# Stores that add onto rows laid beforehand, a fifth list level, and the last weighing on ScalarE, in an attention and mixture-of-experts kernel

## Chip, cores and metric

One Trainium2 chip, one core. The metric is the device time of one execution in microseconds, as the median of three runs.

## What is computed

Four sequences of 1024 tokens with 128 features, float32. A layer norm and an attention block are added onto the tokens, then a layer norm and a routed block of 8 experts, of which each token takes the best two:

```python
x = x + attention(layernorm(x))              # causal softmax, w_q, w_k, w_v, w_o
h = layernorm(x)                             # [4096, 128]
scores = softmax(h @ gate_w.T)               # 8 experts
top_scores, sel = top_k(scores, 2)
y[n, k] = (silu(h[n] @ w1[e]) * (h[n] @ w3[e])) @ w2[e]      # e = sel[n, k], H = 256
out = x + top_scores[:, 0] * y[:, 0] + top_scores[:, 1] * y[:, 1]
```

## The kernel before

**Attention.** The tokens lie in 32 tiles of 128 (`N_TILES`), in the SBUF tensor `X`, which is updated in place. A software pipeline of 32 steps does one tile a step. VectorE's `attend` (L1008) writes x + attention into `X` and raises `x1_rdy`, so `x1_rdy` 4(c+1) means that chunk c of four tiles is final. Every four tiles form a routing group (`GROUPS`, 8 of them). GpSimd's `scatter` (L524) sends each token's normalised row twice, once for each chosen expert, into the DRAM tensor `expert_rows`, where each expert has a stretch of its own: 64 indirect DMAs of 128 rows.

**The list.** Which 128 rows the expert loop takes at each of its steps is worked out on VectorE, on one partition. `LEVELS` names the groups after which rows are counted: the list takes first the whole tiles of rows that are there after group 4, then those after group 6, then the others. So a tile early in the list has only tokens of early groups, and their results are complete early. `list_full` writes the first 32 entries (`NT0`), `list_rest` the other 40 (`NT1`), from arrays `past` and `pasts` of 40 x `SEG` elements, with `SEG` = 8 x (number of levels) = 32. `list_rest` is cut into 7 parts that stand between VectorE's tile steps 8 to 18 (`REST_AT`).

**The expert loop.** 71 steps (`NT`), one for each tile of rows. In step t TensorE multiplies tile t by w1 and w3 (`up`, L747), turns tile t+4 (`pair`, L764), and multiplies the gated tile t-3 by w2 (L768). ScalarE stages the weights (L884) and takes the silu (L889). VectorE (`out_pair`) copies the turned tile, keeps the destinations and weights of tile t+4 in a ring `ycol` of 16 (`keep_places`, L1214, which waits until the store of tile t-12 has landed), weighs the result of tile t-3 into a ring `ysb` of 16 (L1226, `y_rdy`), and multiplies the gate (L1231). GpSimd's `store` (L535) sends `ysb` by an indirect DMA to `choice_rows`: 8192 rows, first those of choice 0 of each token, then those of choice 1, and rows behind them where padding goes. There are 65 stores (`STORED`). The results of the last 6 tiles are not stored: TensorE adds them onto the last three token tiles by a matrix of ones and zeros (`sow`, L691).

**The end.** SyncE's queue, in program order: the loads of rows (L395); `fetch(c)` of chunks 0 to 4, both choices, between the last five loads (L424, two DMAs of 256 KB a chunk); the writes of chunks 0 to 2 to the output (L429); a wait for the stores of the first 63 tiles and the fetches of chunks 5 and 6; a wait for all 65 and half of the last fetch (L346). ScalarE's queue: a wait for all stores, the other half of the last fetch (L346), and the writes of chunks 3 to 6 (L957). VectorE adds the fetched chunks to `X`, first choice 0 and then choice 1 (L1391, one instruction each), those of chunks 0 to 2 between its steps 59 to 64, the others behind the loop; then the sown sums (L1423, L1425) and the last chunk (L1432, L1435). The last writes are at L352.

Of the kernel before, what the change touches and what calls it, by code (L numbers as in the profile page):

```python
# [22 lines left out]
P = 128  # L23
B, S, D = 4, 1024, 128
# [34 lines left out]
ROWS_HALF = K * P * sum(n for _, n in GROUPS[:HALF + 1])  # L59
NT0 = (ROWS_HALF - E * (P - 1)) // P // LANES * LANES  # L60
NEAR = 16
FAR, LATER = 6, 63
SOWN = 3
LEVELS = (HALF, FAR, len(GROUPS) - 1, len(GROUPS) - 1)
SEG = len(LEVELS) * E
NT1 = LISTED - NT0
assert (ROWS_HALF + E * (P - 1)) // P - NT0 <= NEAR
assert (K * P * sum(n for _, n in GROUPS[:FAR + 1]) + E * (P - 1)) // P <= LATER
assert GROUPS[-1][1] > SOWN
N_PARTS = 5  # L70
REST_AT = [8, 9, 10, 12, 14, 16, 18]
# [16 lines left out]
CHUNKS = [(0, 2), (4, 4), (6, 4), (12, 4), (14, 4), (20, 4), (22, 4), (28, 2)]  # L88
N_EARLY, N_LATER = 5, 7
FETCH_AT = [66, 67, 68, 69, 70]  # L90
N_SOON, ADD_AT = 3, [59, 61, 63]
REST_OF = (STORED // OUT_LANES, STORED % OUT_LANES)


def pieces(c):

    a, apart = CHUNKS[c]
    return [(a, FIN)] if apart == 2 and c < NF - 1 else [(a, 2), (a + apart, 2)]
# [13 lines left out]
def build(nc, x, w_q, w_k, w_v, w_o, gate_w, w1, w2, w3, out):  # L112
# [9 lines left out]
    with ctx:  # L122
# [6 lines left out]
        def sem(name):  # L129
            return ctx.enter_context(nc.semaphore(name))  # L130
# [104 lines left out]
        head_mm, step_mm, xT_rdy, sil_rdy, g_rdy = (  # L235
            sem("head_mm"), sem("step_mm"), sem("xT_rdy"), sem("sil_rdy"), sem("g_rdy"))
        ycol_rdy = sem("ycol_rdy")
        Wt_rdy, y_rdy = sem("Wt_rdy"), sem("y_rdy")
        y_zero, low_rdy, lowf_rdy, pick_rdy, sown_mm = (
            sem("y_zero"), sem("low_rdy"), sem("lowf_rdy"), sem("pick_rdy"), sem("sown_mm"))  # L240
        sum2, last0, last1 = sem("sum2"), sem("last0"), sem("last1")
        assert NF - N_EARLY == LAG
        yf_in = [sem(f"yf_in{j}") for j in range(ZF)]
        sum0, sum1, out_done = sem("sum0"), sem("sum1"), sem("out_done")
        N_DESTS = 2 + (NF - 2) // 2
        N_CONST, N_PADS, M_TILES = 6, 11 + K * N_DESTS, LISTED // LANES


        ov = out.rearrange("b (i p) d -> p (b i) d", p=P)

        def is_tile(u):
            return 0 <= u < N_TILES
# [85 lines left out]
        def stores_in(eng, t0, t1):  # L338

            for q in range(OUT_LANES):  # L340
                if len(range(q, t1, OUT_LANES)) > len(range(q, t0, OUT_LANES)):
                    eng.wait_ge(y_out[q], 16 * len(range(q, t1, OUT_LANES)))
# [15 lines left out]
        def _(sp):  # L358
# [16 lines left out]
            for half, w in enumerate((w1, w3)):  # L375
# [4 lines left out]
            sp.wait_ge(pads_rdy, N_PADS)  # L380
            sp.dma_start(xs[E * STRETCH:XS_ROWS, :].rearrange("(j p) c -> p j c", p=P),
                         padrows[:, E:, :]).then_inc(padded, 16)
            for k in range(K):
                sp.dma_start(yv[:, k, LAST, :, :], padrows[:, 0:FIN, 0:D]).then_inc(y_zero, 16)

            def load(m, pads=(), between=False):
                _, firsts = nc.values_load_multi_w_load_instructions(
# [18 lines left out]
            rows_of(range(HALF + 1))  # L406
            sp.wait_ge(list_rdy, 1)
            load(0)
            with sp.Fori(1, M0 - 1) as m:
                load(m)  # L410

# [10 lines left out]
            def fetch(c):  # L422
                for k in range(K):
                    sp.dma_start(yf[:, c, k, :, :], yv[:, k, c, :, :]).then_inc(yf_in[c], 16)  # L424
# [15 lines left out]
                load(m)  # L440
            for m in range(FETCH_AT[0] // LANES, M_TILES):
                load(m, between=True)
            for c in range(N_SOON):
                write(c)
            stores_in(sp, 0, LATER)
            for c in range(N_EARLY, LAST):
                fetch(c)
            stores_in(sp, LATER, STORED)
            fetch_last(sp, 0)
            write_last(sp, 0)  # L450
# [4 lines left out]
        def _(pool):  # L455
# [72 lines left out]
            def store(r, q):  # L528

                pool.wait_ge(y_rdy, r * OUT_LANES + q + 1)  # L530
                if not isinstance(r, int):
                    pool.sem_inc(held, 1)
                    pool.wait_ge(step_mm, r * OUT_LANES + q + 2 + LAG)
                    pool.sem_inc(held, 1)
                nc.gpsimd.indirect_dma_start(  # L535
                    yb, bass.IndirectOffsetOnAxis(ap=ycol[:, q, 0:1].bitcast(u32), axis=0),
                    ysb[:, q, :], None).then_inc(y_out[q], 16)

            waiting = []
            pad_constants()  # L540
# [40 lines left out]
            for n in range(turn, turn + len(waiting) + NT0):  # L581
                after_tile(n)
                if (n - turn) % 5 in (0, 2) and waiting:
                    scatter(*waiting.pop(0))
                elif stored < NT0:
                    if stored == 0:
                        pool.wait_ge(y_zero, 16 * K)
                    store(stored // OUT_LANES, stored % OUT_LANES)
                    stored += 1
            with pool.Fori(NT0 // OUT_LANES, REST_OF[0] - 1) as r:  # L590
# [7 lines left out]
        def _(pe):  # L598
# [85 lines left out]
            def sow(t):  # L684

                n = t - STORED
                pe.wait_ge(y_rdy, t + 1)
                pe.wait_ge(pick_rdy, n + 1)
                for i in range(SOWN):
                    a, at = sown_at(i)  # L690
                    o = mm(a[:, at:at + D], pick[n][:, i * P:(i + 1) * P], ysb[:, t % OUT_LANES, :],  # L691
                           start=n == 0 and at == 0, stop=n == BY_PE - 1, skip_group_check=True)
                if n == BY_PE - 1:
                    o.then_inc(sown_mm, 1)
# [55 lines left out]
            def pair(m, j, w):  # L750

                static, t = isinstance(m, int), m * LANES + j
                b = bank[pair_bank(t if static else LANES + j)]
                used = pair_before(t) if static else t - RING
                if static and used is None:
                    pe.wait_ge(*((xT_rdy, 2 * t + 2) if t < 2 else (x1_rdy, N_TILES - 1) if b is pO else (place_rdy, NG)))
                elif static and used < LAG:
                    pe.wait_ge(xT_rdy, used + LEAD + 1)
                else:
                    pe.wait_ge(y_rdy, used - LAG + 1)  # L760
                if not static or t < LAST_TURN:
                    n = (j + LEAD) % LANES
                    pe.wait_ge(xt_in[n], 16 * (m + (j + LEAD) // LANES + 1))
                    i = nc.tensor.transpose(b[:, 0:P], xt[:, n, 0:D], identf[:, :])  # L764
                if not static or t >= LAG:
                    pe.wait_ge(g_rdy, t - LAG + 1)
                    for c in range(H // P):
                        i = mm(b[:, P:P + D], g[:, (j - LAG) % RING, c * P:(c + 1) * P], w2_sb[:, ds(w + c * D, D)],  # L768
                               start=c == 0, stop=c == H // P - 1)
                i.then_inc(step_mm, 1)  # L770
# [70 lines left out]
        def _(act):  # L841
# [102 lines left out]
                    silu(m, j)  # L944
            w = weights_of(M_TILES - 1, LANES - AHEAD)
            last = NT - (M_TILES - 1) * LANES
            for j in range(last):
                if j + AHEAD < last:
                    stage(M_TILES - 1, j + AHEAD, w[j])
                silu(M_TILES - 1, j)  # L950

            stores_in(act, 0, STORED)
            fetch_last(act, 1)
# [8 lines left out]
        def _(dve):  # L962
# [253 lines left out]
            def out_pair(r, q):  # L1216

                t = r * OUT_LANES + q
                b = bank[pair_bank(t if isinstance(r, int) else OUT_LANES + q % RING)]
                dve.wait_ge(step_mm, t + 1)  # L1220
                if not isinstance(r, int) or t < LAST_TURN:
                    v.tensor_copy(xT[:, (q + LEAD) % RING, :], b[:, 0:P]).then_inc(xT_rdy, 1)
                    keep_places(r + (q + LEAD) // OUT_LANES, (q + LEAD) % OUT_LANES)
                if not isinstance(r, int) or t >= LAG:
                    n = (q - LAG) % OUT_LANES
                    v.tensor_scalar(ysb[:, n, :], b[:, P:P + D], ycol[:, n, 1:2], None, ALU.mult).then_inc(y_rdy, 1)  # L1226

# [152 lines left out]

            pairs = X[:, :, 0:D].rearrange("p (n t) d -> p n t d", t=2)

            def add_choice(c, k):

                a, apart = CHUNKS[c]
                Xc = pairs[:, a // 2:a // 2 + apart // 2 + 1:apart // 2, :, :]
                if k == 0:
                    dve.wait_ge(yf_in[c], 16 * K)
                else:
                    dve.wait_ge(sum0, c + 1)  # L1390
                v.tensor_tensor(Xc, Xc, yf[:, c, k, :, :].rearrange("p (n t) d -> p n t d", t=2),  # L1391
                                ALU.add).then_inc([sum0, sum1][k], 1)

            for t in range(LANES, OUT_LANES + LAG):
                tile_step(0, t)
# [4 lines left out]
                    tile_step(r, q)  # L1400
            for t in range(NT0 + NEAR + LAG, NT):
                tile_step(t // OUT_LANES, t % OUT_LANES)
                for k in range(K):
                    if t - k in ADD_AT:
                        add_choice(ADD_AT.index(t - k), k)
                if t == NT - LEAD - 1:
                    low_places()
                for n in range(2):
                    if STORED <= STORED + 2 * (t - NT + LEAD) + n < NT:
                        picks(STORED + 2 * (t - NT + LEAD) + n)  # L1410
            out_pair(*divmod(NT, OUT_LANES))
            add_choice(N_SOON, 0)
            out_pair(*divmod(NT + 1, OUT_LANES))
            add_choice(N_SOON, 1)
            out_pair(*divmod(NT + 2, OUT_LANES))
            for c in range(N_SOON + 1, LAST):
                for k in range(K):
                    add_choice(c, k)

            n1 = N_TILES - SOWN  # L1420
            dve.wait_ge(sown_mm, 1)
# [37 lines left out]
```

## Time and profile before

| | us |
|---|---|
| median of 3 runs | 239.3 (238.39 to 239.92) |
| the profiled execution's own time | 239.59 |
| its span, first to last instruction | 237.8 |
| TensorE busy | 225.1 (95%) |
| VectorE busy | 187.6 (79%) |
| GpSimd busy | 163.3 (69%) |
| ScalarE busy | 145.8 (61%) |

The profiled execution is 1.8 us longer than its span and 0.3 us over the median. Engines are PE (TensorE), PEld (its weight loads), DVE (VectorE), ACT (ScalarE), POOL (GpSimd) and SP (SyncE). The mean granted clock of TensorE is 0.994 of full speed.

### The profile page before, as it was taken

How to read it: one execution, taken by the hardware profiler on the slowest of the kernel's cores; microseconds unless marked ns; L12 is line 12 of the kernel's file. 1: busy time of each engine (PE TensorE's matmuls, PEld its weight loads, DVE VectorE, ACT ScalarE, POOL GpSimd, SP SyncE). 2: the span in 40 equal slices, each digit the busy share in tenths (PEclk: the TensorE clock that was granted, in tenths of full speed). 3: DMA queues.
4: the chain of work that ended last, by engine and by line, in shares of the span. 5: the costliest groups of instructions: out<-in, count | busy, mean ns of one | idle time of the engine just before them, and what ended most of it. 6: DMA issues, size and time to landing. Idle time of an engine off the chain costs nothing.

```text
span 237.8 us, 6363 instructions
## 1 busy us (share of the span) xinstructions
PE 225.1 (95%) x1794; PEld 206.4 (87%) x1795; DVE 187.6 (79%) x851; ACT 145.8 (61%) x391; POOL 163.3 (69%) x204
## 2 busy tenths in 40 slices
PE   7989999999999999999999999999999999999960
PEld 6978888898799767877999998889999999999960
DVE  2479898879897789977898799957675656699994
ACT  2267787777877757855699665556575656566300
POOL 6523337788888888868577777777777777777700
PEclk9999999999999999999999999999999999999997
DMA  7999801111111111115124425534333333598368
GB/s 224 305 320 335 234 5 36 36 37 46 34 50 36 48 40 41 46 37 136 37 75 108 108 82 129 127 96 124 94 110 103 101 90 102 165 331 274 102 192 276
DMA packets 31978, 28.95 MB, mean 122 GB/s; under 512 B 4152, under 2 KB 26560, under 8 KB 31952
## 3 DMA queue, kind: packets, MB, share of 16 engines
q1 hardware_dynamic: 25216, 18.60, 28.5%
q0 software_dynamic: 4128, 8.59, 10.8%
q10 hardware_dynamic: 2608, 1.45, 2.0%
q8 instruction: 12, 0.20, 0.4%
q14 instruction: 14, 0.11, 0.2%
HBM read 16.34 MB, written 12.29 MB: 120 GB/s over the span
## 4 chain that ended last, share of the span: by engine, by line
PE 79%; POOL 6%; DMA 5%; DVE 3%; ACT 2%; issue 2%; ACTq 1%; POOLq 1%
PE scores L747 12%; PE turned L747 12%; PE scores L619 12%; PE weighed L680 11%; PE scores L768 6%; PE turned L645 5%; POOL expert_rows L524 4%; PE mixed L768 3%; PE weighed L768 3%; PE mixed L634 3%; PE mixed L633 3%; DMA choice_rows<-ysb,ycol 2%; DMA TL<-choice_rows 2%; DMA TL<-L_attn_w_o 2%; PE scores L764 2%
## 5 line engine op out<-in xcount | busy, mean ns | idle before, releaser
L535 POOL DMA_INDIRECT choice_rows<-ysb,ycol x65 | 65.0, 999 | 19.8 <-issue 14.6
L524 POOL DMA_INDIRECT expert_rows<-rows,slots x64 | 64.4, 1007 | 18.2 <-issue 13.2
L884 ACT ACTIVATE Wt<-W 128x512 f32 x71 | 44.1, 625 | 15.7 <-issue 15.7
L747 PE MATMUL scores<-xT,Wt 128*128 128x128 f32 x288 | 38.2, 276 | 0.8 <-issue 0.8
L619 PE MATMUL scores<-XX,TL 128*128 128x512 f32 (+3 forms) x96 | 38.1, 506 | 0.2 <-ACT TL L857 0.2
L680 PE MATMUL weighed<-TL,PT 128*128 128x136 f32 x272 | 37.0, 281 | 0.8 <-DVE X L1008 0.7
L747 PE MATMUL turned<-xT,Wt 128*128 128x128 f32 x280 | 37.1, 275 | 0.0
L747 PEld LDWEIGHTS scores<-xT,Wt 128*128 128x128 f32 x288 | 35.0, 192 | 1.1 <-issue 1.1
L680 PEld LDWEIGHTS weighed<-TL,PT 128*128 128x128 f32 x272 | 33.7, 190 | 1.7 <-issue 1.6
L747 PEld LDWEIGHTS turned<-xT,Wt 128*128 128x128 f32 x280 | 34.1, 192 | 0.0
L996 DVE TENSOR_REDUCE negmax<-scores 128x1 f32<-128x128 f32 (+7 forms) x32 | 23.5, 734 | 5.0 <-PE scores L619 5.0
L873 ACT ACTIVATE Pr<-scores,negmax 128x128 f32<-128x128 f32 (+7 forms) x32 | 23.9, 746 | 3.8 <-DVE negmax L996 3.5
L470 POOL TENSOR_TENSOR rstd<-ve,halves 128x1 f32<-128x1 f32 x32 | 19.2, 601 | 9.4 <-DVE ve L1021 8.9
L857 ACT ACTIVATE TL<-mixed 128x264 f32<-128x264 f32 x31 | 12.1, 391 | 20.8 <-PE mixed L634 20.5
L768 PE MATMUL scores<-w_sb,g 128*128 x156 | 24.1, 277 | 0.1
L867 ACT ACTIVATE PT<-turned 128x512 f32<-128x512 f32 (+3 forms) x48 | 21.9, 492 | 2.4 <-PE turned L645 2.4
L619 PEld LDWEIGHTS scores<-XX,TL 128*128 128x128 f32 x96 | 15.7, 191 | 8.6 <-issue 7.6
L889 ACT ACTIVATE sil<-turned 128x256 f32<-128x256 f32 x35 | 13.5, 385 | 15.1 <-PE scores L768 9.2
L645 PE MATMUL turned<-identf,Pr 128*128 128x128 f32 x144 | 21.1, 273 | 0.3 <-ACT Pr L873 0.3
L768 PEld LDWEIGHTS scores<-w_sb,g 128*128 128x128 f32 x156 | 20.5, 191 | 0.6 <-issue 0.3
L889 ACT ACTIVATE sil<-scores 128x256 f32<-128x256 f32 x36 | 13.6, 378 | 10.1 <-PE scores L768 6.1
L1231 DVE TENSOR_TENSOR g<-sil,scores 128x256 f32<-128x256 f32 x36 | 14.8, 412 | 5.5 <-ACT sil L889 5.5
(182 smaller groups left out, 456.1 us busy)
## 6 DMA issues: line engine op xcount, KB each, us to landing
xt<-expert_rows SPq DMA_DIRECT2D x71, 66.0 KB
TL<-choice_rows SPq DMA_DIRECT2D x15, 256.0 KB, 3.9
W<-L_ffn_w SPq DMA_DIRECT2D x2, 1024.0 KB, 9.7
out<-X ACTq DMA_DIRECT2D x9, 128.0 KB
choice_rows<-ysb,ycol POOLq DMA_INDIRECT x65, 2.3
X<-L_attn_in_features SPq DMA_DIRECT2D x2, 512.0 KB, 7.5
expert_rows<-rows,slots POOLq DMA_INDIRECT x64
out<-X SPq DMA_DIRECT2D x5, 128.0 KB
```

The costliest lines, as they stand in the source:

```text
L524: nc.gpsimd.indirect_dma_start(xs, bass.IndirectOffsetOnAxis(ap=slots[:, u, k:k + 1], axis=0), rows[:, u % ROWS_RING, k, :], None).then_in ...
L535: nc.gpsimd.indirect_dma_start(yb, bass.IndirectOffsetOnAxis(ap=ycol[:, q, 0:1].bitcast(u32), axis=0), ysb[:, q, :], None).then_inc(y_out[ ...
L619: i = mm(pS[u % 2][:, c:c + n * P], TL[:, token_tile(u), 0:P], keys, start=not last, stop=True, skip_group_check=last)
L645: i = nc.tensor.transpose(pT[n % 2][:, kt % 4 * P:(kt % 4 + 1) * P], Pr[:, u % 2, kt * P:(kt + 1) * P], identf[:, :])
L680: i = mm(weighed(u), PT[:, u % 2, kt * P:(kt + 1) * P], TL[:, first_key(u) + kt, P:], start=kt == 0, stop=kt == blocks(u) - 1)
L747: mm(bank[2 + j % RING][:, c * P:(c + 1) * P], Wt[:, j % RING, c * P:(c + 1) * P], xT[:, j % RING, :], start=True, stop=True)
L768: i = mm(b[:, P:P + D], g[:, (j - LAG) % RING, c * P:(c + 1) * P], w2_sb[:, ds(w + c * D, D)], start=c == 0, stop=c == H // P - 1)
L867: copy(PT[:, u % 2, 4 * c * P:4 * c * P + w], pT[n % 2][:, 0:w], ACT.Copy).then_inc(pt_ev, 1)
L873: copy(Pr[:, u % 2, 0:w], pS[u % 2][:, 0:w], ACT.Exp, bias=negmax[:, u:u + 1], scale=1.0, accum_out=rowsum[:, u:u + 1]).then_inc(p_rdy, 1)
L884: copy(Wt[:, j % RING, :], W[:, ds(w * (SET // WIDE), SET)], ACT.Copy).then_inc(Wt_rdy, 1)
L889: copy(sil[:, j % RING, :], bank[2 + j % RING][:, 0:H], ACT.Silu).then_inc(sil_rdy, 1)
L996: v.tensor_reduce(negmax[:, u:u + 1], pS[u % 2][:, 0:blocks(u) * P], AX.X, ALU.max, negate=True).then_inc(max_rdy, 1)
```

## The change

- **Stores that add.** `store` gets `compute_op=ALU.add`: the DMA adds onto the row that is there. For this SyncE lays rows beforehand. The residual of chunks 0 to 6 goes from `X` into the rows of choice 0 as soon as attention has finished a chunk (`lay_residual`, 13 DMAs, 1.75 MB in all), chunks 0 to 4 ahead of the first row load, 5 and 6 behind the first eight. Zeros go into the rows of choice 1, the padding rows and the last chunk's choice 0 (3 DMAs of 1 MB and one of 256 KB, where there were two of 256 KB). GpSimd's first store waits for all of these.
- **One addition a chunk.** `add_choices` writes `X` = fetched choice 0 + fetched choice 1, one instruction where there were two.
- **A list level.** `LEVELS` gets group 5 (`MID`): `SEG` is 40, the arrays in `list_rest` have 1600 elements instead of 1280, and chunk 5 is complete once 55 tiles are stored (`SOONER`).
- **Order at the end.** SyncE fetches chunk 5 right behind the last load and a wait for 55 tiles, then writes chunks 0 to 4, waits for 63 tiles and fetches chunk 6. ScalarE's queue writes chunks 5 and 6 alone.
- **ScalarE weighs sown tiles.** The results of tiles 65 to 70 are weighed by ScalarE (`weigh_sown`, `ys_rdy`), ahead of its wait for the stores and its half of the last fetch. VectorE's `out_pair` has nothing left to do in those steps.

```diff
+MID, SOONER = 5, 55
-LEVELS = (HALF, FAR, len(GROUPS) - 1, len(GROUPS) - 1)
+LEVELS = (HALF, MID, FAR, len(GROUPS) - 1, len(GROUPS) - 1)
-N_SOON, ADD_AT = 3, [59, 61, 63]
+N_SOON, ADD_AT = 5, [59, 61, 63, 65, 67]
...
+        ZERO_ROWS = (E + SPARE) * P
+        ZERO_AT = range(N_TOK, YB_ROWS, ZERO_ROWS)
...
-            for k in range(K):
-                sp.dma_start(yv[:, k, LAST, :, :], padrows[:, 0:FIN, 0:D]).then_inc(y_zero, 16)
+            sp.dma_start(yv[:, 0, LAST, :, :], padrows[:, 0:FIN, 0:D]).then_inc(y_zero, 16)
+            for n in ZERO_AT:
+                sp.dma_start(yb[n:n + ZERO_ROWS, :].rearrange("(j p) d -> p j d", p=P),
+                             padrows[:, :, 0:D]).then_inc(y_zero, 16)
+
+            def lay_residual(c):
+
+                sp.wait_ge(x1_rdy, (c + 1) * FIN)
+                for n, z in pieces(c):
+                    i = 0 if n == CHUNKS[c][0] else 2
+                    sp.dma_start(yv[:, 0, c, i:i + z, :], X[:, n:n + z, 0:D]).then_inc(y_base, 16)
+
+            for c in range(HALF + 1):
+                lay_residual(c)
...
             load(0)
+            for c in range(HALF + 1, LAST):
+                lay_residual(c)
...
+            stores_in(sp, 0, SOONER)
+            fetch(MID)
             for c in range(N_SOON):
                 write(c)
-            stores_in(sp, 0, LATER)
-            for c in range(N_EARLY, LAST):
-                fetch(c)
+            stores_in(sp, SOONER, LATER)
+            fetch(FAR)
...
-                    ysb[:, q, :], None).then_inc(y_out[q], 16)
+                    ysb[:, q, :], None, compute_op=ALU.add).then_inc(y_out[q], 16)
...
-                        pool.wait_ge(y_zero, 16 * K)
+                        pool.wait_ge(y_zero, 16 * (1 + len(ZERO_AT)))
+                        pool.wait_ge(y_base, 16 * sum(len(pieces(c)) for c in range(LAST)))
...
+            def weigh_sown(t):
+
+                at = t + LAG
+                act.wait_ge(ycol_rdy, t + 1)
+                act.wait_ge(step_mm, at + 1)
+                copy(ysb[:, t % OUT_LANES, :], bank[pair_bank(at)][:, P:P + D], ACT.Copy,
+                     scale=ycol[:, t % OUT_LANES, 1:2]).then_inc(ys_rdy, 1)
...
+                if t - LAG >= STORED:
+                    weigh_sown(t - LAG)
+            for t in range(NT - LAG, NT):
+                weigh_sown(t)
...
-            def add_choice(c, k):
+            def add_choices(c):
...
-                if k == 0:
-                    dve.wait_ge(yf_in[c], 16 * K)
-                else:
-                    dve.wait_ge(sum0, c + 1)
-                v.tensor_tensor(Xc, Xc, yf[:, c, k, :, :].rearrange("p (n t) d -> p n t d", t=2),
-                                ALU.add).then_inc([sum0, sum1][k], 1)
+                dve.wait_ge(yf_in[c], 16 * K)
+                y0, y1 = (yf[:, c, k, :, :].rearrange("p (n t) d -> p n t d", t=2) for k in range(K))
+                v.tensor_tensor(Xc, y0, y1, ALU.add).then_inc(sum1, 1)
```

## Rows read from the trace of the kernel before

**Rows 1.** The page: the span, and the chain that ended last, by engine.
```profile
span 237.8 us, 6363 instructions
...
PE 79%; POOL 6%; DMA 5%; DVE 3%; ACT 2%; issue 2%; ACTq 1%; POOLq 1%
```

**Rows 2.** The chain in order of time, its last pieces: start, length, what.
```profile
224.39 4.85 DMA choice_rows<-ysb,ycol
...
229.26 4.30 DMA TL<-choice_rows
...
234.84 0.42 DVE X L1435
```

**Rows 3.** Timeline of GpSimd: start, length, instruction, idle before it.
```profile
123.20 1.03 POOL L524 DMA_INDIRECT expert_rows<-rows,slots  x1 [0.19 <-issue]
...
132.12 0.96 POOL L535 DMA_INDIRECT choice_rows<-ysb,ycol  x1 [0.31 <-DVE ysb L1226]
...
138.43 2.08 POOL L535 DMA_INDIRECT choice_rows<-ysb,ycol  x1 [0.30 <-issue]
...
142.07 1.97 POOL L535 DMA_INDIRECT choice_rows<-ysb,ycol  x1 [0.30 <-issue]
...
145.61 0.95 POOL L524 DMA_INDIRECT expert_rows<-rows,slots  x1 [0.30 <-issue]
...
224.39 1.03 POOL L535 DMA_INDIRECT choice_rows<-ysb,ycol  x1 [0.30 <-issue]
```

**Rows 4.** Timeline of VectorE, read as Rows 3.
```profile
107.58 0.36 DVE L1008 SCALAR_TENSOR_TENSOR X<-weighed,rinv,X 128x136 f32<-128x136 f32 x1 [0.31 <-issue]
...
138.20 1.47 DVE L1128 TENSOR_TENSOR past<-cum,iotat 1x1280 f32<-1x1280 f32 x1
...
141.73 1.48 DVE L1138 TENSOR_TENSOR pasts<-past,step 1x1280 f32<-1x1280 f32 x1
...
144.96 1.47 DVE L1142 TENSOR_REDUCE e_of<-past 1x40 f32<-1x1280 f32 x1
...
156.83 0.17 DVE L1214 COPY ycol<-xt 128x2 f32<-128x2 f32 x1 [2.03 <-DMA choice_rows<-ysb,ycol]
...
220.75 0.35 DVE L1226 TENSOR_SCALAR ysb<-scores,ycol 128x128 f32<-128x128 f32 x1
...
228.11 0.35 DVE L1226 TENSOR_SCALAR ysb<-scores,ycol 128x128 f32<-128x128 f32 x1 [0.17 <-PE scores L768]
228.38 4.07 DVE L1391 TENSOR_TENSOR X<-X,TL 128x512 f32<-128x512 f32 x6
```

**Rows 5.** Instructions and waits on the rows of the choices (their tile), all of them.
```profile
L535 POOL DMA_INDIRECT choice_rows<-ysb,ycol x65: 954/958/2077, 132.1 to 224.4; - x65
...
  DVE ycol L1214: 6.1, 10
...
DMA to landing us min/median/max: 2.2/2.6/5.2
```

**Rows 6.** The scatters of the other indirect form: shortest, median and longest in ns.
```profile
L524 POOL DMA_INDIRECT expert_rows<-rows,slots x64: 954/961/1208, 36.6 to 154.5; - x64
```

**Rows 7.** Timeline of TensorE, the first part of two steps in a row.
```profile
206.16 1.06 PE L747 MATMUL turned<-xT,Wt 128*128 128x128 f32 x8
...
207.61 1.06 PE L747 MATMUL turned<-xT,Wt 128*128 128x128 f32 x8
```

**Rows 8.** Timeline of the queues that issue DMAs, SyncE first, then ScalarE.
```profile
224.15 1.79 SPq L424 DMA_DIRECT2D TL<-choice_rows  x4
...
229.69 4.40 ACTq L957 DMA_DIRECT2D out<-X  x8
```

**Rows 9.** DMA issues from 220 us on: GB/s in 40 slices of 0.45 us, size and time to landing.
```profile
GB/s 246 244 0 0 146 0 0 146 0 0 146 64 278 323 291 351 278 241 323 196 132 32 55 36 36 168 346 344 359 344 343 344 340 344 344 288 320 74 0 0
...
TL<-choice_rows SPq DMA_DIRECT2D x5, 256.0 KB, 3.7
```

**Rows 10.** One line of ScalarE: copies of 128x128 out of PSUM.
```profile
L846 ACT ACTIVATE XX<-scores x32: 259/278/298, 10.2 to 103.6; 128x128 f32<-128x128 f32 x32
```

More of the change, by code:

```diff
@@ L67 @@
 assert (ROWS_HALF + E * (P - 1)) // P - NT0 <= NEAR
-assert (K * P * sum(n for _, n in GROUPS[:FAR + 1]) + E * (P - 1)) // P <= LATER
+assert all((K * P * sum(n for _, n in GROUPS[:l + 1]) + E * (P - 1)) // P <= most for l, most in ((MID, SOONER), (FAR, LATER)))
 assert GROUPS[-1][1] > SOWN
@@ L237, in build @@
         ycol_rdy = sem("ycol_rdy")
-        Wt_rdy, y_rdy = sem("Wt_rdy"), sem("y_rdy")
+        Wt_rdy, y_rdy, ys_rdy = sem("Wt_rdy"), sem("y_rdy"), sem("ys_rdy")
         y_zero, low_rdy, lowf_rdy, pick_rdy, sown_mm = (
@@ L241, in build @@
         sum2, last0, last1 = sem("sum2"), sem("last0"), sem("last1")
-        assert NF - N_EARLY == LAG
+        assert MID == HALF + 1 == N_EARLY and FAR == NF - 2
         yf_in = [sem(f"yf_in{j}") for j in range(ZF)]
-        sum0, sum1, out_done = sem("sum0"), sem("sum1"), sem("out_done")
+        y_base, sum1, out_done = sem("y_base"), sem("sum1"), sem("out_done")
         N_DESTS = 2 + (NF - 2) // 2
@@ L249, in build @@
         ov = out.rearrange("b (i p) d -> p (b i) d", p=P)
+        ZERO_ROWS = (E + SPARE) * P
+        ZERO_AT = range(N_TOK, YB_ROWS, ZERO_ROWS)
+        assert (YB_ROWS - N_TOK) % ZERO_ROWS == 0
         def is_tile(u):
@@ L686, in sow @@
                 n = t - STORED
-                pe.wait_ge(y_rdy, t + 1)
+                pe.wait_ge(ys_rdy, n + 1)
                 pe.wait_ge(pick_rdy, n + 1)
@@ L758, in pair @@
                     pe.wait_ge(xT_rdy, used + LEAD + 1)
+                elif not static or used - LAG < STORED:
+                    pe.wait_ge(y_rdy, used - LAG + 1)
                 else:
-                    pe.wait_ge(y_rdy, used - LAG + 1)
+                    pe.wait_ge(ys_rdy, used - LAG - STORED + 1)
                 if not static or t < LAST_TURN:
@@ L946, in _ @@
             last = NT - (M_TILES - 1) * LANES
+            def weigh_sown(t):
[4 more added lines that the diff above has]
+                     scale=ycol[:, t % OUT_LANES, 1:2]).then_inc(ys_rdy, 1)
             for j in range(last):
+                t = (M_TILES - 1) * LANES + j
                 if j + AHEAD < last:
@@ L1223, in out_pair @@
                     keep_places(r + (q + LEAD) // OUT_LANES, (q + LEAD) % OUT_LANES)
-                if not isinstance(r, int) or t >= LAG:
+                if not isinstance(r, int) or LAG <= t < STORED + LAG:
                     n = (q - LAG) % OUT_LANES
@@ L1402, in _ @@
                 tile_step(t // OUT_LANES, t % OUT_LANES)
-                for k in range(K):
-                    if t - k in ADD_AT:
-                        add_choice(ADD_AT.index(t - k), k)
+                if t in ADD_AT:
+                    add_choices(ADD_AT.index(t))
                 if t == NT - LEAD - 1:
@@ L1410, in _ @@
                         picks(STORED + 2 * (t - NT + LEAD) + n)
[L1411 to L1418, printed above, removed]
+            for c in range(N_SOON, LAST):
+                add_choices(c)
             n1 = N_TILES - SOWN
```

## The prediction

> **What bounds the kernel now.** I read the page first. Its chain gives 79% of the span to PE [rows 1], but a share over the whole span says nothing of the end, so I then read the chain in order of time. Its last pieces name no TensorE work [rows 2]: the 65th store starts at 224.39 us and takes 4.85 us to land, the last fetch follows at 229.26 and takes 4.30, then come the last additions (to 235.26) and a write that ends the span at 237.8.
>
> What sets the start of the last store? VectorE had its data ready at 220.75 + 0.35 = 221.1 us [rows 4], 3.3 us before. So it waited for GpSimd. The timeline of GpSimd shows why: from 123.20 to 224.39 + 1.03 = 225.42 it issues 80 indirect DMAs, 15 scatters and all 65 stores, without one idle gap over 0.31 us [rows 3], and 102.2 / 80 = 1.28 us each, where one takes 0.96 and the gap that the profile calls issue takes 0.30. TensorE's step is 207.61 - 206.16 = 1.45 us [rows 7]. GpSimd fell behind while it had scatters beside stores, and has not quite caught up when the last store goes. **GpSimd's queue is the path of the last store**, and every nanosecond that a store gains costs 65 at the end. TensorE's path lies beside it: the last result of the loop is weighed at 228.11 us [rows 4].
>
> A second contact: the ring of 16. VectorE waited 10 times, 6.1 us in all, for a store to land before it could keep new places [rows 5], the longest 2.03 us, to 156.83 [rows 4]. So a store that lands later moves VectorE, and then TensorE, from there on.
>
> **Part 1, stores that add: GpSimd's time.** The trace holds no adding DMA. Its two indirect forms, rows of 528 and of 512 bytes, take the same 0.961 and 0.958 us [rows 5, 6], so the number of rows seems to set the time, not the bytes, and the rows stay 128. Lower bound 0: the same instruction with one more field has nothing to make it shorter. Upper bound: two DMAs during VectorE's long list operations show how much of the instruction is real work (next part): about 0.84 of its 0.96 us. Were this work half as long again, the extra would be 0.42 us. I take 0, the value of the two rows nearest to it, and keep the rest as a rival, for it is multiplied by 65.
>
> **Part 2, stores that add: landing.** A store lands 2.2 us after its start at the quickest (the median of 2.6 in that row holds the fetches too) [rows 5]; this DMA must now also read the DRAM row before it writes. A fetch, which reads DRAM, lands in 3.7 us [rows 9], of which 256 KB at 344 GB/s are 0.75, so 3.0. The extra lies between 0 and 3.0 - 2.2 = 0.8, or 1.6 if read and write follow each other wholly. I take 0.8. It hits twice: the last store lands 0.8 later, and VectorE's ring wait ends 0.8 later, which TensorE follows, since GpSimd's pace (1.26) is faster than TensorE's (1.45) only afterwards.
>
> **Part 3, the list level.** `list_rest` has four operations of 1280 elements at 1.47 us [rows 4]; at 1600 they take about 1.84, so VectorE has 4 x 0.37 + one more small operation, 1.7 us, more to do between 138 and 153 us. This lies in front of the 2.03 us that VectorE waited for a store, and is covered by it. But two of the four hold GpSimd up: the store at 138.43 starts inside the TENSOR_TENSOR of 138.20 to 139.67 and takes 2.08 us, the one at 142.07 inside that of 141.73 to 143.21 and takes 1.97, while the scatter at 145.61, inside the TENSOR_REDUCE of 144.96, takes 0.95 [rows 3, 4]. Both delayed stores end 0.83 to 0.84 us after VectorE's instruction does. So the two-input list operations each add their extension to the GpSimd queue: 2 x 0.37 = **+0.7 us** on the path of the last store. It depends on where a store happens to start in them: with a store every 1.26 us the sum lies between -1.3 and +1.2.
>
> **Part 4, laying rows.** Zeros: 3.25 MB behind the weight loads, at 344 GB/s [rows 9] 9.4 us of DMA time, in the early attention, where no load is waited for after that. Residuals: 13 DMAs of 128 or 256 KB over 80 us. The last of them needs 28 finished tiles, which attention has at 107.58 + 0.36 [rows 4]; the first store starts at 132.12 [rows 3], so its new waits cost nothing with 24 us of cover. On SyncE the row loads behind `lay_residual` wait for the expert loop's first steps anyway. I take 0 for all of it.
>
> **Part 5, the additions and ScalarE's weighing.** VectorE loses 7 additions of 4.07 / 6 = 0.68 us, 4.8 us [rows 4], and six weighings. None is on the chain: the additions behind the loop end at 232.45, before the last fetch lands at 233.56. Worth nothing by itself. ScalarE pays some 0.28 us a weighing [rows 10] for VectorE's 0.35 and has the time. But one thing moves: ScalarE issues its half of the last fetch **behind** its last weighing, which waits for TensorE's last product. Before, that product was weighed on another engine. So the last fetch now also waits for TensorE's path.
>
> **Part 6, the tail's transfers.** Before, 1 MB of fetches started at 224.15 [rows 8], beside the last store, which took 4.85 us instead of 2.2; the slices show the burst from 225.4 to 229 us [rows 9]. Now half of it, chunk 5, is fetched eight stores earlier. At 344 GB/s 0.5 MB are 1.5 us that the last store need not share. The writes on ScalarE's queue fall from 1 MB to 0.5 MB; the first 0.5 MB still run beside the last fetch, so of the 4.30 us I take off 0.4.
>
> **The sum.** The last store starts 0.7 later (part 3), at 225.1, and lands after 4.85 - 1.5 + 0.8 = 4.15, at 229.2, as before. TensorE's path: the wait at 156.83 ends 0.7 + 0.8 = 1.5 us later, TensorE with it; its last product is done at about 228.1 + 1.5 = 229.6, weighed by 229.9, and ScalarE's half of the last fetch goes at 229.95, against 229.26. It lands after 3.9, at 233.85 against 233.56. So the span grows by 0.3 us, to 238.1: the gain of part 6 is eaten by parts 2, 3 and 5. Profiled time 239.59 + 0.3 = 239.9; the median of the runs was 0.3 under the profiled one, so **239.6 us**. With the low ends (no extra landing, a favourable place for the two stores), the last fetch goes at about 228.6 and the time is 238.0; with the high ones (1.6 and 1.2, TensorE 2.8 later, the fetch at 231.25, minus 0.4) it is 241.0.
>
> **Rival A, GpSimd pays for the add.** Place: each of the 65 stores of the back-to-back queue. The last store decides again as soon as it lands after ScalarE's last weighing, a margin of 0.75 us, so from 0.75 / 65 = 12 ns a store. Price: 239.6 + 65 d - 0.75. With d = 0.07 us, the step between the 0.96 and 1.03 rows [rows 3], 243.4; with d = 0.25, the longest scatter of 1.208 [rows 6], 255; with d = 0.42, 266. Against: the two forms that are equal; for: the 0.84 us of real work must contain whatever is written for each row. The Trainium skill (Collectives: The Full Stack, on the DMA's adding unit) says that such an add takes two reads, and that two read descriptors are emitted for each piece in place of one. By that rule the work per row would be nearer to three parts than two, which is the 266 us end; no row here shows it.
>
> **Rival B, all goes well.** The add costs nothing anywhere and the list operations miss the stores: 238.0 as above, or 237.6 if the fetches land in 3.3. More than 1% would need the last fetch to be issued before 227.2, and TensorE's last product at 228.1 forbids it.
>
> **Rival C, adds that land slowly.** Each of the 16 DMA engines serves 8 rows of a store. Were reading and writing back not overlapped, landing could grow by several us; each us beyond mine moves TensorE and the end by one: 3 us give 242.
>
> **Chances.** What a measurement of this kernel can tell from no change is about 1%. Forecast 0.50, at 238.0 to 241.0; A 0.28; B 0.12; C 0.10. Less than 237.6 I hold for 0.07, by something I don't see. A spreads from 242 to 266, more of it low, so up to 252 takes in all but about 0.14. Range 237.6 to 252. Faster by over 1% (under 236.9) 0.10; within 0.57; slower (over 241.7) 0.33, from A, most of C and a little of the forecast.
>
> **What the profile after would show.** GpSimd's line of the store: median 0.96 us (right) or more (rival A). Landing: 3.0 at the quickest in place of 2.2. Stores or scatters near 138 and 142 us of some 2.4 us. Two fetches at about 225 us instead of four, a last store that lands in some 4.1 us. ScalarE's half of the last fetch issued after SyncE's. VectorE idle before the last additions. I am wrong if the store line is longer, if VectorE waits for landings all through the loop, or if the first store waits for laid rows.

## The result, and the profile after

The changed kernel takes **277.75 us** (276.5 to 278.51, 4 runs) against 239.24 of the kernel before: ratio 1.158, 95% interval 1.153 to 1.163, 38.5 us slower. My 239.6 and the range to 252 were wrong.

The page of the kernel after; section 5's columns are line, engine, instruction, tiles and count, then busy us and mean ns, then the idle time before it and what ended most of it:

```profile
span 276.4 us, 6390 instructions
...
q0 software_dynamic: 11408, 8.59, 21.4%
...
PE 38%; DMA 20%; POOL 16%; issue 13%; DVE 9%; ACT 2%; POOLq 1%; SPq 0%; DVEq 0%
...
L555 POOL DMA_INDIRECT choice_rows<-ysb,ycol x65 | 101.8, 1566 | 19.8 <-issue 14.0
...
L1251 DVE COPY ycol<-xt 128x2 f32<-128x2 f32 x71 | 12.4, 179 | 43.2 <-DMA choice_rows<-ysb,ycol 43.2
```

The store has become L555. It is the same instruction with the add, its mean is 1566 ns, and TensorE's share of the chain falls from 79% [rows 1] to 38%. VectorE waits 43.2 us for stores to land, where it waited 6.1 [rows 5].

Timeline of GpSimd after (the 1st, the 33rd and the last store):

```profile
133.70 1.62 POOL L555 DMA_INDIRECT choice_rows<-ysb,ycol  x1 [0.30 <-DVE ysb L1263]
...
203.81 1.55 POOL L555 DMA_INDIRECT choice_rows<-ysb,ycol  x1 [0.30 <-issue]
...
263.82 1.55 POOL L555 DMA_INDIRECT choice_rows<-ysb,ycol  x1 [0.30 <-issue]
```

All stores of the changed kernel, by their tile:

```profile
L555 POOL DMA_INDIRECT choice_rows<-ysb,ycol x65: 1554/1554/1902, 133.7 to 263.8; - x65
...
DMA to landing us min/median/max: 3.2/3.3/6.7
```

The median went from 958 [rows 5] to 1554 ns, **0.596 us more for each**. From the first store to the last it was 224.39 - 132.12 = 92.3 us [rows 3] and is now 263.82 - 133.70 = 130.1, 37.9 more; 64 x 0.596 = 38.1. The gap before each is 0.30 as before, and no gap between the first store and the last is over 0.31: the queue is back to back from end to end. So the size of the loss is all but explained; the first store also starts 1.6 us later, and the last one lands 0.7 us sooner after its start. TensorE's mean granted clock fell too, from 0.994 to 0.966, but it is 1.00 from 133 to 204 us, where the first half of the loss arises, so the clock is not what sets it.

The end of the chain in order of time, after:

```profile
263.82 4.13 DMA choice_rows<-ysb,ycol
...
267.97 4.45 DMA TL<-choice_rows
...
273.69 0.42 DVE X L1462
```

It has the shape of [rows 2], 39.4 us later: 4.85 us of landing have become 4.13, and 4.30 of the last fetch 4.45.

### The profile page after: what moved, and what is told of

It is laid out like the page before. It is cut to its first block, busy times and chain, and to the rows that moved or that the text cites. A ratio compares the mean times of both kernels' runs of the same rounds, so it can differ in the third digit from the quotient of the medians.

```text
span 276.4 us, 6390 instructions
## 1 busy us (share of the span) xinstructions
PE 238.0 (86%) x1795; PEld 211.4 (76%) x1796; DVE 184.3 (67%) x840; ACT 148.8 (54%) x397; POOL 201.6 (73%) x204
## 3 DMA queue, kind: packets, MB, share of 16 engines
q0 software_dynamic: 11408, 8.59, 21.4%
## 4 chain that ended last, share of the span: by engine, by line
PE 38%; DMA 20%; POOL 16%; issue 13%; DVE 9%; ACT 2%; POOLq 1%; SPq 0%; DVEq 0%
DMA choice_rows<-ysb,ycol 16%; POOL choice_rows L555 11%; PE scores L640 8%; PE weighed L701 8%; POOL expert_rows L544 4%; PE turned L666 4%; DMA TL<-choice_rows 3%; PE scores L768 3%; PE turned L768 3%; PE mixed L655 2%; PE mixed L654 2%; PE scores L791 1%; DMA TL<-L_attn_w_o 1%; DVE ysb L1263 1%; PE mixed L728 1%
## 5 line engine op out<-in xcount | busy, mean ns | idle before, releaser
L555 POOL DMA_INDIRECT choice_rows<-ysb,ycol x65 | 101.8, 1566 | 19.8 <-issue 14.0
L544 POOL DMA_INDIRECT expert_rows<-rows,slots x64 | 66.0, 1031 | 18.2 <-issue 13.5
L768 PE MATMUL scores<-xT,Wt 128*128 128x128 f32 x288 | 40.3, 285 | 5.6 <-issue 5.6
L768 PEld LDWEIGHTS scores<-xT,Wt 128*128 128x128 f32 x288 | 36.7, 199 | 6.8 <-issue 6.8
L1251 DVE COPY ycol<-xt 128x2 f32<-128x2 f32 x71 | 12.4, 179 | 43.2 <-DMA choice_rows<-ysb,ycol 43.2
L640 PE MATMUL scores<-XX,TL 128*128 128x512 f32 (+3 forms) x96 | 38.1, 506 | 0.2 <-ACT TL L880 0.2
L791 PE MATMUL scores<-w_sb,g 128*128 x156 | 26.6, 294 | 4.5 <-DVE g L1268 4.0
L791 PEld LDWEIGHTS scores<-w_sb,g 128*128 128x128 f32 x156 | 21.3, 198 | 8.6 <-issue 8.6
```

Of the source, the lines that this page charges most:

```text
L544: nc.gpsimd.indirect_dma_start(xs, bass.IndirectOffsetOnAxis(ap=slots[:, u, k:k + 1], axis=0), rows[:, u % ROWS_RING, k, :], None).then_in ...
L555: nc.gpsimd.indirect_dma_start(yb, bass.IndirectOffsetOnAxis(ap=ycol[:, q, 0:1].bitcast(u32), axis=0), ysb[:, q, :], None, compute_op=ALU. ...
L640: i = mm(pS[u % 2][:, c:c + n * P], TL[:, token_tile(u), 0:P], keys, start=not last, stop=True, skip_group_check=last)
L768: mm(bank[2 + j % RING][:, c * P:(c + 1) * P], Wt[:, j % RING, c * P:(c + 1) * P], xT[:, j % RING, :], start=True, stop=True)
```

## The experiments

They ran in three sessions, on the chips that the record numbers 7, 4 and 7; it doesn't number the chip of the result above ("first session" below). In these three sessions the kernel before takes 264 to 267 us (medians of 17, 29 and 29 runs) instead of 239. The kernels of one session are compared with its own before; why the level differs is looked at under "before_again".

### Only the add taken out, and only the add put in

plain_stores:

```diff
-                    ysb[:, q, :], None, compute_op=ALU.add).then_inc(y_out[q], 16)
+                    ysb[:, q, :], None).then_inc(y_out[q], 16)
```

> The kernel after with one thing undone: the stores copy instead of adding, everything else (laying rows, list level, order at the end, ScalarE's weighing) stays. It leaves out the residual and overwrites the laid rows. Theory 1, GpSimd's time per adding store (1.554 us against 0.958 in the two traces, 65 stores in a back-to-back queue, 38.7 us): 238 to 241 us, store line back at 0.96 us. Rival, the other parts carry a share of the 38.5 us: 245 us or more.

Measured: 264.35 us against 264.03 of before, ratio 1.000 (0.997 to 1.003). The store's median is back at 962 ns. Laying rows, the fifth level, the new order and ScalarE's weighing cost nothing that can be measured where before takes 264. The absolute 238 to 241 was missed, since before itself is at 264 here.

zeros_and_add, the kernel before with:

```diff
-            for k in range(K):
-                sp.dma_start(yv[:, k, LAST, :, :], padrows[:, 0:FIN, 0:D]).then_inc(y_zero, 16)
+            for n in range(0, YB_ROWS, (E + SPARE) * P):
+                sp.dma_start(yb[n:n + (E + SPARE) * P, :].rearrange("(j p) d -> p j d", p=P),
+                             padrows[:, :, 0:D]).then_inc(y_zero, 16)
...
-                        pool.wait_ge(y_zero, 16 * K)
+                        pool.wait_ge(y_zero, 16 * (YB_ROWS // ((E + SPARE) * P)))
...
-                    ysb[:, q, :], None).then_inc(y_out[q], 16)
+                    ysb[:, q, :], None, compute_op=ALU.add).then_inc(y_out[q], 16)
```

> The kernel before with one thing done: all rows of the choices are zeroed beforehand and the stores add; VectorE's additions, list, fetches and writes as before. Theory 1: 239.2 + 65 x 0.596 = 278 us, give or take 2. Rival, the other parts carry a share: under 270.

Measured: 280.03 us, ratio 1.060 (1.051 to 1.068). The add alone brings the time to that of the whole change, and to the time expected from a before of 239, in a session where before is at 264. There before is only 16 us faster. So the queue of adding stores gives nearly one time whatever before takes, and the 264 is another limit, which it overtakes.

### Is it the length of the queue, or the landing?

longer_queue, the kernel before with plain stores and

```diff
+                if not isinstance(r, int) or r * OUT_LANES + q > 0:
+                    pool.wait_ge(spent, r * OUT_LANES + q)
+                nc.gpsimd.tensor_tensor(extra[:, 0:1], ve1[:, 0:1], halves[:, 0:1], ALU.pow).then_inc(spent, 1)
                 nc.gpsimd.indirect_dma_start(
```

> The kernel before with plain stores, and one GpSimd instruction of about 0.6 us (a power of 128x1 elements, result unused) ahead of each store. Theory 1, what counts is how long GpSimd's queue is, not what the DMA does: about 239.2 + 65 x 0.6 = 278 us, with VectorE waiting some 40 us for landings although a store lands as fast as before. Rival, theory 2, the adding DMA lands later (median 3.3 us against 2.3) and the ring of 16 hands that on: 239 to 241 us, hardly any wait.

Measured: 278.5 us, ratio 1.054 (1.046 to 1.062). GpSimd's timeline, and from the view of the stores' tile who waited for it:

```profile
200.93 0.57 POOL L538 TENSOR_TENSOR extra<-ve,halves 128x1 f32<-128x1 f32 x1
201.69 1.03 POOL L539 DMA_INDIRECT choice_rows<-ysb,ycol  x1 [0.20 <-POOL extra L538]
...
203.52 1.03 POOL L539 DMA_INDIRECT choice_rows<-ysb,ycol  x1 [0.19 <-POOL extra L538]
```
```profile
  DVE ycol L1218: 41.0, 42
```

A store every 203.52 - 201.69 = 1.83 us, nearly as after (1.86), without any add; and VectorE "waits for the DMA" 41.0 us in 42 pieces. That is the sign that the changed kernel shows (43.2), and it comes here without an adding DMA: the store it waits for was late in the queue. (The trace has no landing times of these stores.) With the back-to-back queue of the kernel after, in which no store waits for a landing, the landing theory is out.

small_dose, the same with `nc.gpsimd.memset(extra[:, :], 0.0)` on 128x128 elements in place of the power:

> The kernel before with a small GpSimd instruction (a memset of 128x128, about 0.2 us) ahead of each store. Where the queue is the bound (before at 239), every 0.1 us that the instruction adds to a store's turn costs 6.5 us: some 10 to 15 us. Where before is at 264, the queue has slack of about 25 us beside it, so nothing or up to 5 us.

Measured: 267.99 us against 267.08, ratio 1.002 (0.999 to 1.005). Two stores in a row were 205.07 - 203.72 = 1.35 us apart:

```profile
203.72 0.97 POOL L539 DMA_INDIRECT choice_rows<-ysb,ycol  x1 [0.16 <-POOL extra L538]
...
205.07 0.97 POOL L539 DMA_INDIRECT choice_rows<-ysb,ycol  x1 [0.17 <-issue]
```

A turn is 0.09 us longer than the usual 1.26, not 0.2 as expected, since the gap before the store shrinks. That is some 6 us of queue, and they disappear (at most 1.3 us by the interval): here the queue has idle time.

### What an add costs, form by form

prices, the kernel before with 24 DMAs behind its last store:

```diff
+            def form(dest, at, n, c, **kw):
+                nc.gpsimd.iota(place[:, :], [[1, 1]], base=at, channel_multiplier=1).then_inc(placed, 1)
...
+                nc.gpsimd.indirect_dma_start(
+                    dest, bass.IndirectOffsetOnAxis(ap=place[0:n, 0:1], axis=0),
+                    ysb[0:n, 0, 0:c], None, **kw).then_inc(formed, 16)
+                pool.wait_ge(formed, 16 * n_form[0])
+            for rep in range(3):
+                form(wide_rows, 0, P, D)
+                form(wide_rows, 0, P, D, compute_op=ALU.add)
...
```

> The kernel before with 24 indirect DMAs behind the last store, one at a time, to DRAM rows of their own: copying and adding, each at 128, 64 and 32 rows of 512 bytes and at 128 rows of 128 bytes, three times. The total is of no interest. If the 0.6 us is per row (a descriptor more for each), the add costs about 0.3 more at 64 rows, 0.15 at 32, and 0.6 at 128 short rows. If it is fixed for an instruction, 0.6 everywhere. If it goes by bytes, 0.15 at the short rows.

One run, and its total (341.64 us) says nothing. The second of the three rounds, copy and add in turns: 128 rows, 64, 32, and 128 short rows. The third is within 0.01 us of it; in the first the pair at 128 rows took 1.06 and 1.80.

```profile
281.32 1.00 POOL L608 DMA_INDIRECT wide_rows<-ysb,place  x1 [0.46 <-POOL place L605]
283.65 0.12 POOL L605 IOTA place<- 128x1 uint32 x1 [1.33 <-DMA wide_rows<-ysb,place]
284.05 1.57 POOL L608 DMA_INDIRECT wide_rows<-ysb,place  x1 [0.28 <-POOL place L605]
287.32 0.12 POOL L605 IOTA place<- 128x1 uint32 x1 [1.69 <-DMA wide_rows<-ysb,place]
287.71 0.93 POOL L608 DMA_INDIRECT wide_rows<-ysb,place  x1 [0.28 <-POOL place L605]
...
290.45 1.46 POOL L608 DMA_INDIRECT wide_rows<-ysb,place  x1 [0.40 <-POOL place L605]
...
293.95 0.89 POOL L608 DMA_INDIRECT wide_rows<-ysb,place  x1 [0.28 <-POOL place L605]
...
296.44 1.36 POOL L608 DMA_INDIRECT wide_rows<-ysb,place  x1 [0.28 <-POOL place L605]
...
299.71 1.01 POOL L608 DMA_INDIRECT slim_rows<-ysb,place  x1 [0.28 <-POOL place L605]
...
302.32 1.58 POOL L608 DMA_INDIRECT slim_rows<-ysb,place  x1 [0.28 <-POOL place L605]
```

The add costs 0.57, 0.53, 0.47 and 0.57 us. Bytes don't matter, and rows hardly: a straight line through 32 and 128 rows gives about 0.44 us for the instruction and 0.001 for a row. A copy is alike, 0.85 and 0.0012. So it is neither of my first two cases, but nearest to a fixed price. The next instruction waits for the landing, so the trace shows that too: at 128 rows the copy lands 283.65 - 281.32 = 2.33 us after its start and the add 287.32 - 284.05 = 3.27.

### The rest of the change by itself

parts_without_add is the kernel after without the add, without `lay_residual`, with the two zeroing DMAs of before, and with

```diff
-                v.tensor_tensor(Xc, y0, y1, ALU.add).then_inc(sum1, 1)
+                v.tensor_tensor(Xc, Xc, y0, ALU.add).then_inc(y_base, 1)
+                dve.wait_ge(y_base, c + 1)
+                v.tensor_tensor(Xc, Xc, y1, ALU.add).then_inc(sum1, 1)
```

> The kernel after without stores that add and without laying rows, with two additions a chunk as before: what is left of the change is the list level, chunk 5 fetched behind the loads, and ScalarE's weighing. By my sum for these parts (0.7 us on GpSimd's queue, 1.5 us less crowding of the last store) within 1% of before. Rival: the earlier fetch and the emptier tail show, 1% to 2% faster. Rival: VectorE's longer list operations cost TensorE, 1% slower.

Measured: 264.3 us, ratio 0.999 (0.996 to 1.001). The same kernel once more, in the third session:

> The kernel after without adding stores and laid rows, as in parts_without_add. On a chip at 264, again within 0.5% of before. On one at 239, where GpSimd's queue sets the last store, my sum says within 1% of before, 1 us faster at best since ScalarE's half of the last fetch waits for its last weighing.

Measured: 266.45 us against 267.08, ratio 0.998 (0.995 to 1.000). No difference either time. Since GpSimd's queue isn't the limit in these sessions, this doesn't test my sum for a before at 239.

level_alone, the kernel before with `LEVELS = (HALF, MID, FAR, ...)` and nothing else:

> The kernel before with the fifth list level and nothing else. GpSimd's two DMAs that start inside the two-input list operations take 0.3 to 0.4 us longer than the 2.08 and 1.97 us of before if they start at the same place in them; time within 0.5% of before.

Measured: 265.36 us, ratio 1.002 (0.999 to 1.005). VectorE's timeline, then GpSimd's:

```profile
147.13 1.81 DVE L1128 TENSOR_TENSOR past<-cum,iotat 1x1600 f32<-1x1600 f32 x1
...
151.02 1.81 DVE L1138 TENSOR_TENSOR pasts<-past,step 1x1600 f32<-1x1600 f32 x1
```
```profile
147.69 2.08 POOL L535 DMA_INDIRECT choice_rows<-ysb,ycol  x1 [0.30 <-issue]
...
151.35 2.33 POOL L524 DMA_INDIRECT expert_rows<-rows,slots  x1 [0.30 <-issue]
```

1280 to 1600 elements take 1.81 us (I had worked out 1.84). Both DMAs again end 0.83 to 0.85 us after the VectorE instruction in which they start (148.94 to 149.77, 152.83 to 153.68), so what the wait costs goes by the place of the start. The second starts 0.33 us into its instruction, as the 1.97 did (0.34), and is 0.36 longer, as expected; the first starts 0.56 in, where it was 0.23, and takes 2.08 again.

### How two limits combine

first_32_add, the kernel before with all rows zeroed as in zeros_and_add and

```diff
-                    ysb[:, q, :], None).then_inc(y_out[q], 16)
+                    ysb[:, q, :], None, **({"compute_op": ALU.add} if isinstance(r, int) and r < NT0 // OUT_LANES else {})).then_inc(y_out[q], 16)
```

> The kernel before with all rows zeroed beforehand, where only the first 32 stores add. Theory 1: GpSimd's queue grows by 32 x 0.6 = 19 us. Where the queue is the bound (239 us before) that gives 258; where something else gives 264 already, most of it disappears in GpSimd's idle time and the result is 264 to 268. Rival, that every adding store costs its 0.6 us whatever the queue: before + 19 on either chip.

Measured: 272.95 us, ratio 1.031 (1.027 to 1.036), 5 us above what I expected. From the timelines of GpSimd, the time between the starts of the 1st and 33rd store and of the 33rd and 65th, in us:

| kernel | 1st to 33rd | 33rd to 65th |
|---|---|---|
| before, first session | 51.4 | 40.9 |
| before_again | 61.2 | 53.1 |
| first_32_add | 70.3 | 51.6 |
| zeros_and_add | 70.0 | 61.0 |
| longer_queue | 70.2 | 59.4 |
| after, first session | 70.1 | 60.0 |
| after_again | 71.2 | 60.1 |

I had added up the queue over the whole loop (258 us) and compared it with 264. But the longer of the two limits holds **in each stretch by itself**: 70.3 where stores add, 51.6 where they don't. A queue's slack in the second half doesn't pay for its excess in the first. The columns also show the price once more: 32 turns of 1.86 are 59.5, of 1.26 they are 40.3.

### Why before takes 264 there

before_again is the kernel before, unchanged.

> The kernel before, unchanged, for its trace on the chip that gave 264 us where the first had given 239. Theory 1 says that GpSimd's queue alone gives 239 us, so what makes 264 must lie beside it: store line at 0.96 us, GpSimd idle between stores. If GpSimd's instructions are themselves longer there, theory 1 is wrong on this chip.

Measured: 264.46 us, on chip 4 and not, as the expectation has it, on the chip of the experiments above (7). And before_third in the last session, on chip 7:

> The kernel before, unchanged, a third time: 239 us if this chip is like the first, 264 if it is like the two of the other experiments. At 264 TensorE again has pauses in the middle of a group of matmuls, and VectorE and ScalarE wait up to 4 us for its announcements; at 239 it has none.

Measured: 266.67 us. GpSimd's stores are as short as ever (medians 962 and 958 ns); GpSimd waits. The granted clock is 0.997 in before_again, so the clock isn't the reason. TensorE's timeline in before_again, then VectorE's and ScalarE's:

```profile
162.64 0.27 PE L764 MATMUL mixed<-identf,xt 128*128 128x128 f32 x1
163.54 0.71 PE L768 MATMUL mixed<-w_sb,g 128*128 x4 [0.63 <-issue]
...
164.98 0.27 PE L764 MATMUL scores<-identf,xt 128*128 128x128 f32 x1
165.09 0.61 PE L768 MATMUL scores<-w_sb,g 128*128 x4
166.23 1.13 PE L747 MATMUL scores<-xT,Wt 128*128 128x128 f32 x8 [0.53 <-issue]
```
```profile
164.71 0.41 DVE L1231 TENSOR_TENSOR g<-sil,scores 128x256 f32<-128x256 f32 x1
167.53 0.29 DVE L1222 COPY xT<-mixed 128x128 f32<-128x128 f32 x1 [2.40 <-remote]
```
```profile
167.53 0.39 ACT L889 ACTIVATE sil<-turned 128x256 f32<-128x256 f32 x1 [2.89 <-remote]
```

VectorE idles for 2.4 us until 167.53 for a product ("mixed") whose matmuls by the trace had ended by 164.25. ScalarE is released at the same moment. The waits of VectorE's copy and ScalarE's silu for TensorE's products (us, times, longest), in before_again and then in the kernel before of the first session:

```profile
ACT sil L889 <- PE scores L768: 32.4, 14, 4.3
DVE xT L1222 <- PE scores L768: 22.2, 10, 4.1
```
```profile
ACT sil L889 <- PE scores L768: 15.3, 26, 1.0
DVE xT L1222 <- PE scores L768: 6.3, 14, 0.5
```

In before_third the longest of these waits are 3.4 and 3.2 us, and 4.5 and 4.2 where the profile names no engine ("remote"). My reading is that TensorE's announcements arrive late, and that TensorE, which may be only a few steps ahead, then pauses. It isn't shown: the ends of matmuls are modelled in a trace, and "remote" leaves open what the engines waited for. In the first session there is nothing of this, and TensorE is busy for 45.0 of the 45 us from 160 to 205, against 38.0 in before_again. By the second column above, a step of the loop is 53.1 / 32 = 1.66 us against TensorE's 1.45 [rows 7]. That slower step is the limit at 264. What causes it stays open, whether the chip or something else that differed between the sessions; the kernels are the same to the last instruction, and no kernel here could change it.

after_again, the kernel after, unchanged:

> The kernel after, unchanged. By theory 1 GpSimd's queue of adding stores is the bound on every chip, so 277 to 281 us whatever before is here: 1.16 times a before of 239, 1.06 times one of 264. Rival, the loss is a share that any chip adds to its own before: 264 + 38 = 302.

Measured: 280.59 us against 267.08, ratio 1.048 (1.042 to 1.054). This is in the range expected and far from the rival's 302. The changed kernel takes 278 us in the first session and 281 here, so the same change costs 16% in the one and 5% in the other.

## Why the prediction was wrong

- **What bounds the kernel** was read rightly: GpSimd's queue is the path of the last store, and what a store gains in length counts 65 times. 0.596 x 65 = 38.7 us, measured 38.5. longer_queue shows it without an add. (By the trace the queue from 123.20 on holds 79 DMAs, 14 scatters and 65 stores, not 80; nothing hangs on the one.)
- **Part 1 failed**, the term for GpSimd's time, on the value that I took and on its bound: I had 0 with at most 0.42 us, and 0.596 was measured. I took 0 for the add's time on GpSimd, since two forms of copy cost the same; they differ in bytes alone and say nothing of a computing form. And my upper bound of 0.42 us rested on the reading that 0.84 us of a store is work for its 128 rows. By prices, a copy of 32 rows still takes 0.89, so the rows are about 0.15 of it; the rest is fixed, and so is most of the add's 0.57. The Trainium skill's rule that a collective's add emits two read descriptors where a copy emits one (Collectives: The Full Stack, on the bandwidth ceiling) pointed the right way. The trace agrees only in kind: the software queue has 11408 packets where it had 4128 (`q0 software_dynamic: 4128, 8.59, 10.8%` before), which is 32 for each of 129 indirect DMAs, so with 32 for each of the 64 scatters a store now has (11408 - 2048) / 65 = 144. That is 4.5 times as many, not twice, for the same 8.59 MB, and the price here is hardly one for each row. What in the instruction takes the fixed time, no run shows.
- **The weighing of rival A** failed too. With a multiplier of 65 on an unknown, no row of the trace excluded a large value, and 0.28 with a range to 252 was too little. A's own end, 266, lay 12 us short. The chances didn't agree with each other either: less than 237.6 had 0.07, and under 236.9, which is part of it, had 0.10.
- **Part 2**: a store lands 3.2 us after its start at the quickest, where it was 2.2. Of the 1.0 us, 0.6 is the longer instruction, which leaves 0.4 for the DMA; I had 0.8. In prices, one DMA at a time, it is 3.27 against 2.33, of which 0.57 is the instruction. VectorE's ring wait came, not once with 1.5 us but 46 times, as the queue never caught up.
- **Part 3**, VectorE's two-input instructions holding up GpSimd's DMAs, held: in the kernel after, two scatters of 1.57 and 1.73 us stand there, and end 0.87 and 0.88 us behind VectorE. The size of the sum is chance of place, as said.

```profile
139.57 1.81 DVE L1165 TENSOR_TENSOR past<-cum,iotat 1x1600 f32<-1x1600 f32 x1
...
143.46 1.81 DVE L1175 TENSOR_TENSOR pasts<-past,step 1x1600 f32<-1x1600 f32 x1
```
```profile
140.68 1.57 POOL L544 DMA_INDIRECT expert_rows<-rows,slots  x1 [0.30 <-issue]
...
144.42 1.73 POOL L544 DMA_INDIRECT expert_rows<-rows,slots  x1 [0.30 <-issue]
```

- **Part 4** held: the first store starts at 133.70 against 132.12, but 1.2 of these 1.6 us are there at VectorE's first attention result (19.95 us against 18.77), before any row is laid (the first such DMA goes at 24.0), and the first store goes 0.30 us behind the scatter before it, so it waited for no laid row. plain_stores has all of the laying and costs nothing where before takes 264.
- **Parts 5 and 6** are hidden in the kernel after: SyncE's and ScalarE's halves of the last fetch go together at 267.97, with the last store's landing; ScalarE's last weighing was over 9 us earlier. What part 5 feared does come in the kernels without the add. In parts_without_add ScalarE's half goes only behind its last weighing, 3 us after SyncE's (251.7), and it ends the chain:

```profile
254.17 0.37 ACT L969 ACTIVATE ysb<-scores,ycol 128x128 f32<-128x128 f32 x1 [0.75 <-PE scores L784]
254.79 0.38 ACTq L351 DMA_DIRECT2D TL<-choice_rows  x1
```

  It is paid for there by what part 5 called worth nothing. In before_again both halves go at 252.4, but VectorE's additions behind the loop last until 257.8 and end the chain in its place. The two nearly cancel: the times are within 0.5% of before. For a before of 239 no run shows the balance.
- **Rival B** and **rival C** are out for this kernel: B would have the add free, and landing isn't what costs. Whether the rest of the change would gain anything on a before of 239 stays open; where before takes 264, plain_stores gains nothing.

## What to carry to other kernels

When one engine's queue of equal instructions is back to back up to the end, the first question to any change of that instruction is its own length on that engine, times the count; if no row has the new form, the range has to be as wide as that product, and a run of the form by itself comes before any design that needs it. A wait "for the DMA" can be a wait for the engine that issues it: look when that DMA was issued before you call it slow. And limits are to be compared stretch by stretch, not as totals.

## What the runs showed of the hardware

- An indirect DMA that adds takes GpSimd 0.47 to 0.60 us more than one that copies, nearly whatever its rows (32 to 128) and bytes, and by the counts of the software queue has 144 packets in place of 32 at 128 rows.
- A GpSimd DMA that starts inside a VectorE TENSOR_TENSOR with both inputs in SBUF ended 0.83 to 0.88 us after it (six cases, in before, level_alone and after); the scatter that started inside a TENSOR_REDUCE took 0.95, as others do.
- One and the same kernel took 239 us in one session and 264 to 267 in three others, with a mean granted clock of 0.994 in the fast one's trace and of 0.997 and 0.990 in before_again's and before_third's; in before_again VectorE and ScalarE waited up to 4.3 us at a time for TensorE's products (1.0 in the first session), and the cause stays open.
